# Start of a four-layer sequence kernel: the first batch's order, halved stack loads, and the second batch's transform ahead of the score units

## The reference, cut to what matters

```python
# layer 1 (stage A), per batch
q, k, v = u @ Wq.T + bq, u @ Wk.T + bk, u @ Wv.T + bv     # transposed to channel x time
q, k = dwconv(q), dwconv(k)                               # 3 taps
kv = k * v
y = irfft(rfft(kv) * rfft(ssm_kernel))[..., :L]
y = (y + kv * D_skip) * q
x = layernorm(u + y.T @ Wo.T + bo)
# layer 2 (stages C and B), per batch
attn = causal_softmax_attention(rmsnorm(x, ln1), Wq, Wk, Wv, Wo)    # 16 heads of 16
mod = 0.1 * tanh(attn @ A)
h = rmsnorm(x, ln2)
gate = silu(h @ W_in.T + mod * (h @ A) @ B)
x = layernorm(x + x + (gate * (h @ W_up.T)) @ W_down.T)
# layer 3 (stage D): cumulative sum of k*v, times q, projected; layernorm; layer 4: top 6 of 64 experts
```

## Time and profile before

| | us |
|---|---|
| median of three runs | 1110.93 |
| lowest, highest | 1100.03, 1113.92 |
| the profiled execution | 1113.63 |
| its span, first to last instruction | 1110.3 |
| TensorE busy in it | 1015.0 (91%) |
| mean granted TensorE clock | 0.964 |

### The profile page before, as it was taken

One profiled execution on the slowest core, in us unless ns is written; L12 is line 12 of the kernel. 1 busy time (PEld: TensorE's weight loads), 2 busy tenths in 40 slices (PEclk: granted clock), 3 DMA queues, 4 the chain that ended last, 5 costly groups with the idle time before them and its releaser, 6 DMA issues. The chain is left out here.

```text
span 1110.3 us, 20976 instructions
## 1 busy us (share of the span) xinstructions
PE 1015.0 (91%) x6531; PEld 826.7 (74%) x6531; DVE 618.6 (56%) x2071; ACT 338.1 (30%) x1035; POOL 458.9 (41%) x516
## 2 busy tenths in 40 slices
PE   8888999999999999999998998788998989898986
PEld 6665877877878878878776776576786868686874
DVE  4535466676776766667665563544344444444356
ACT  1235254263353453452542620011011101010333
POOL 2123142282291471551642814414455445455612
PEclk9899999999999999999999999898899989898999
DMA  9497590511412214004004101497496776768286
GB/s 364 137 253 146 150 282 11 129 40 52 94 47 79 58 44 115 32 34 119 30 26 119 50 10 49 172 347 266 140 296 210 226 229 201 232 201 272 81 317 222
DMA packets 102919, 163.28 MB, mean 147 GB/s; under 512 B 26865, under 2 KB 77010, under 8 KB 100434
## 3 DMA queue, kind: packets, MB, share of 16 engines
q1 hardware_dynamic: 85394, 113.31, 35.9%
q0 software_dynamic: 12288, 33.96, 8.2%
q10 hardware_dynamic: 5184, 15.36, 3.8%
HBM read 139.32 MB, written 61.87 MB: 181 GB/s over the span
## 5 line engine op out<-in xcount | busy, mean ns | idle before, releaser
L1154 ACT ACTIVATE prob<-bank,nmx 128x128 f32<-128x128 f32 (+1 forms) x256 | 104.9, 431 | 67.5 <-DVE nmx L1423 64.8
L612 POOL TENSOR_TENSOR prob<-prob,rec 128x512 f32<-128x512 f32 x96 | 99.6, 1045 | 54.5 <-DVE rec L1429 53.8
L1423 DVE TENSOR_REDUCE nmx<-bank 128x2 f32<-128x512 f32 (+1 forms) x96 | 65.3, 686 | 53.0 <-PE bank L843 43.1
L637 POOL DMA_INDIRECT x_rows<-x_copy,desti x84 | 85.2, 1015 | 18.3 <-issue 18.2
L1147 ACT ACTIVATE probT<-bank 128x512 f32<-128x512 f32 x96 | 58.0, 604 | 60.3 <-PE bank L707 58.0
L903 PE MATMUL bank<-h2T,w_up 128*128 128x256 f32 x256 | 66.4, 382 | 0.0
L905 PE MATMUL bank<-h2T,w_in 128*128 128x256 f32 x256 | 65.7, 379 | 0.0
L304 POOL TENSOR_TENSOR spare<-ones_row 128x1 f32<-128x1 f32 x49 | 9.4, 191 | 136.2 <-DVE d_cs L1654 75.0
L707 PE MATMUL bank<-cst,prob 128*128 128x128 f32 x384 | 60.2, 280 | 6.0 <-ACT probT L1147 4.5
L627 POOL TENSOR_TENSOR products<-z,products 128x512 bf16<-128x512 f32 x8 | 9.3, 1157 | 133.8 <-ACT products L1135 133.8
L971 PE MATMUL bank<-x3T,sh_gu 128*128 128x256 f32 (+1 forms) x192 | 49.3, 401 | 10.7 <-DVE sact L1540 6.6
(11 more groups left out here) (387 smaller groups left out, 2515.7 us busy)
## 6 DMA issues: line engine op xcount, KB each, us to landing
w_in<-in_e_w SPq DMA_DIRECT2D x20, 448.0 KB
w_up<-in_e_w SPq DMA_DIRECT2D x20, 448.0 KB
w_down<-in_e_w SPq DMA_DIRECT2D x20, 448.0 KB
products<-in_e_w SPq DMA_DIRECT2D x20, 448.0 KB
prob<-in_e_w SPq DMA_DIRECT2D x20, 448.0 KB
probT<-in_e_w SPq DMA_DIRECT2D x20, 448.0 KB
actT<-in_e_w SPq DMA_DIRECT2D x20, 448.0 KB
x_rows<-sgt SPq DMA_DIRECT2D x1, 8320.0 KB, 28.5
```

The source lines that it names most:

```text
L612: pool.tensor_tensor(p, p, r, ALU.mult).then_inc(S["b_scaled"], 1)
L637: pool.indirect_dma_start(x_rows, bass.IndirectOffsetOnAxis(ap=desti[:, n:n + 1].bitcast(U32), axis=0), rows[:, n // TOPK, :], None).then_ ...
L1154: i = act.activation(prob[:, u % PROBS, h * w:(h + 1) * w], psum(u % 2, h * w, (h + 1) * w), ACT.Exp, bias=nmx[:, u, h:h + 1], accum_out=s ...
L1423: dve.tensor_reduce(nmx[:, u, 0:512 // w], bank[:, u % 2, :].rearrange("p (h k) -> p h k", k=w), AX, ALU.max, negate=True).then_inc(S["b_m ...
```

## The change

Four things, all in the turns.

1. In the first batch VectorE combines the products into `Yre` and `Yim` right after making them, and GpSimd adds `bo` as soon as the forward transform is done. The first two operations on the matrix B (A3s) move behind the gating, the other two (A3t) behind C1. The idle matmuls become 2 before A5, 11 before C1, 2 before C2 and 8 before u0.
2. In the first batch `stack_up` loads each stack in halves of the heads: the first halves of q and of k (semaphore `st_half`), then the second halves. u0 waits for the first halves, u2 for the second.
3. In the second turn A2, A3a and A3b stand ahead of u0 on TensorE, with ScalarE's A2, VectorE's A3p and GpSimd's A3p moved likewise; A5 stands ahead of u7 instead of behind it.
4. In the six turns 2 to 7 VectorE's D5p stands ahead of its C2.

```diff
@@ ORDER, of some lists only
             "first": {
-                "dve": """A3p Aq A3s A4y A4z A5n A5o A6n A6o C1 C1s C2 Zk Zq""",
+                "dve": """A3p Aq A4y A4z A3s A5n A5o A6n A6o C1 A3t C1s C2 Zk Zq""",
...
             "second": {
-                "act": """u0 A2 u1 u2 u3 u4 u5 u6 u7 u8 u9 u10 u11 u12 u13 u14 B6a B6b C1 f0 f1 C2 f2 f3 C2v f4 f5 f6 Z1k f7 Z1v Z1q Z2""",
+                "act": """A2 u0 u1 u2 u3 u4 u5 u6 u7 u8 u9 u10 u11 u12 u13 u14 B6a B6b C1 f0 f1 C2 f2 f3 C2v f4 f5 f6 Z1k f7 Z1v Z1q Z2""",
@@ stack_up, SyncE
+            def half_of(t, half):
+                n = HEADS // KT * KT * L // 2
+                return t[:, half * n:(half + 1) * n]
...
                     for j, a in enumerate(first_parts):
                         parts = 3 if j < 2 else 2
-                        sp.dma_start(stack[n][j * 3 * HD:(j * 3 + parts) * HD].rearrange("p h k l -> p (h k l)"),
-                                     rows(t, a, a + parts)).then_inc(S[f"st_{n}"], 16)
+                        if first(b):
+                            sp.dma_start(half_of(stack[n][j * 3 * HD:(j * 3 + parts) * HD].rearrange("p h k l -> p (h k l)"), 0),
+                                         half_of(rows(t, a, a + parts), 0)).then_inc(S["st_half"], 16)
+                        else:
+                            sp.dma_start(stack[n][j * 3 * HD:(j * 3 + parts) * HD].rearrange("p h k l -> p (h k l)"),
+                                         rows(t, a, a + parts)).then_inc(S[f"st_{n}"], 16)
+                if first(b):
+                    for n, t, first_parts in (("q", q_parts, (0, 0, 0)), ("k", k_parts, (1, 2, 0))):
+                        for j, a in enumerate(first_parts):
+                            parts = 3 if j < 2 else 2
+                            sp.dma_start(half_of(stack[n][j * 3 * HD:(j * 3 + parts) * HD].rearrange("p h k l -> p (h k l)"), 1),
+                                         half_of(rows(t, a, a + parts), 1)).then_inc(S[f"st_{n}"], 16)
@@ A3, GpSimd
-                pool.wait_ge(S["a_pr"], b + 1)
-                pool.tensor_tensor(Yre, pr[0], pr[1], ALU.subtract).then_inc(S["a_Y"], 1)
-                pool.tensor_tensor(Yim, pr[2], pr[3], ALU.add).then_inc(S["a_Y"], 1)
-                if first(b):
+                if first(b):
+                    pool.wait_ge(S["a_X"], 2)
                     pool.wait_ge(S["ld_u"], 32)
+                else:
+                    pool.wait_ge(S["a_pr"], b + 1)
+                    pool.tensor_tensor(Yre, pr[0], pr[1], ALU.subtract).then_inc(S["a_Y"], 1)
+                    pool.tensor_tensor(Yim, pr[2], pr[3], ALU.add).then_inc(S["a_Y"], 1)
@@ scores, TensorE
                 if u == 0:
+                    need(pe, "b_act", b * FT)
                     if first(b):
-                        idle(22, 7)
-                    need(pe, "b_act", b * FT)
+                        idle(8, 7)
+                        pe.wait_ge(S["st_half"], 96)
+                if u == (2 if first(b) else 0):
                     pe.wait_ge(S["st_q"], (b + 1) * 48)
                     pe.wait_ge(S["st_k"], (b + 1) * 48)
@@ A3, VectorE
                 i.then_inc(S["a_pr"], 1)
+                if first(b):
+                    dve.wait_ge(S["a_pr"], 1)
+                    dve.tensor_tensor(Yre, pr[0], pr[1], ALU.subtract).then_inc(S["a_Y"], 1)
+                    dve.tensor_tensor(Yim, pr[2], pr[3], ALU.add).then_inc(S["a_Y"], 1)
```

More of the change, by code:

```diff
@@ L281, in build @@
             "a_q a_k a_v a_q_out a_k_out a_v_out a_qc a_kc a_kv a_kvT a_kvT_out a_X a_pr a_Y a_y a_z a_o a_r a_x1 "
[L282 removed]
+            "b_xn b_hT b_h1 b_h2 b_xT b_q b_k b_v b_first b_rest b_second b_third st_qw st_kw st_half st_q st_k b_v_out b_s b_max b_exp b_rec b_scaled b_pT b_pT_out b_pv b_mixed "
             "b_mod b_tanh b_mh b_gu b_gt b_act b_dn b_r b_x2 "
@@ L349, in build @@
                 "act": """u0 D1 u1 u2 D2k u3 u4 u5 u6 u7 u8 u9 D4 u10 S0 u11 S1 D4m u12 S2 u13 u14 B6a B6b C1 f0 f1 f2 C2 C2v f3 f4 f5 f6 Z1k f7 Z1v Z1q Z2""",
-                "dve": """u0 u1 u2 A3p u3 u4 D2v D2w u5 u6 D3n A4y u7 A4z D3o u8 u9 A5n u10 S0 A5o u11 A6n S1 D4m u12 A6o S2 B6b D4t SD C1 f0 D4k f1 f2 C2 f3 f4 D5p D4w D5h f5
+                "dve": """u0 u1 u2 A3p u3 u4 D2v D2w u5 u6 D3n A4y u7 A4z D3o u8 u9 A5n u10 S0 A5o u11 A6n S1 D4m u12 A6o S2 B6b D4t SD C1 f0 D4k f1 f2 D5p C2 f3 f4 D4w D5h f5
                         f6 Zk f7 Zq B8""",
@@ L794, in A5 @@
                 if first(b):
-                    idle(4, 7)
+                    idle(2, 7)
                 pe.wait_ge(S["a_z"], b * 2 + 2)
@@ L807, in C1 @@
                 if first(b):
-                    idle(8, 7)
+                    idle(11, 7)
                 pe.wait_ge(S["b_xn"], b + 1)
@@ L1347, in split_b, with split_rest @@
                     cs.link(dve.tensor_tensor(b_rest, b_b, b_part[0], ALU.subtract))
+            def split_rest(b):
+                if first(b):
                     cs.link(dve.tensor_copy(b_part[1], b_rest))
@@ L1613, in DTb @@
                 cr.link(dve.tensor_copy(expert_of.rearrange("p (c k) -> p k c", k=2), psum3(6)[:, :, 0:P]))
-            turns(dve, "dve", {"DTa": DTa, "DTb": DTb, "Zq": conv("q", q_sb, qc), "Aq": conv("q", q_sb, qc), "Zk": conv("k", k_sb, kc), "A3p": A3, "A3s": split_b, "C1s": stack_b, "A4y": gated(0), "A4z": gated(1), "A5n": A5, "A5o": A5o,
+            turns(dve, "dve", {"DTa": DTa, "DTb": DTb, "Zq": conv("q", q_sb, qc), "Aq": conv("q", q_sb, qc), "Zk": conv("k", k_sb, kc), "A3p": A3, "A3s": split_b, "A3t": split_rest, "C1s": stack_b, "A4y": gated(0), "A4z": gated(1), "A5n": A5, "A5o": A5o,
                         "A6n": A6, "A6o": A6o, "C1": C1, "C2": C2, **{f"u{u}": unit(u) for u in range(UNITS + 1)},
```

1 line of the change is left out of this document (removed), and 6 rows, old and new, of the table ORDER.

## The result

The changed kernel takes 1100.0 us, the median of 20 runs (1085.67 to 1108.58), against 1106.32 us of 20 runs of the kernel before. The ratio is 0.991, with a 95% interval of 0.988 to 0.994, or 10 us (6.9 to 13.3) of the kernel before's time; it leaves out executions more than 1.5% above the fastest of their kernel, 8 of the changed kernel's 20, and over all 20 of each the medians lie 6.3 us apart, a ratio of 0.994. So the gain is some 6 to 10 us. The forecast was 1099, 12 us less and no change beyond 2%. The profiled execution took 1098.68 us, with a span of 1096.8 us against 1110.3.

The account below looks back on a forecast made before the run. TensorE bounds steady turns; the first 68 us are a chain of dependent steps. Gains of 4.9 us at C1, 7.5 at u0, 11.8 at the inverse transform and 12.0 at f0 are cumulative: 1110.9 - 12 = 1099 us, range 1088 to 1109.

Parts of the forecast that it names:

- Convolution and combination: First batch up to the gating: combination until 24.2, convolution until 26.8, projection at about 29.1; its end 4.9 us earlier.
- From C1 to the stores: First batch: q's rest at 43.1 to 43.8, k's rest 6.2 us earlier, stores at about 45.5 instead of 51.72.
- The stacks: Loads ahead of u0: u0 at 60.5 instead of 67.95, 7.5 us earlier; halves worth only 1.2 us; u2 at 63.4.
- halves cost as much as wholes: Rival: second halves land at 75.5 and u2 waits for them, so nothing is gained, 1111 us; chance 0.06.
- The units: Second turn: ScalarE alone paces u0 to u4; inverse transform at 67.6, 11.8 us earlier; f0 at 93.0, 12.0 us earlier.
- Only the start counts: Rival: the units lose the transform as filler and wait; 7.5 us stay, 4.3 do not come, 1103.5 us; chance 0.15.
- 4.3 of them from this part: Second turn's units: of 11.8 us gained at the inverse transform, 4.3 come from moving the transform ahead of u0.
- A low clock around the transform: Rival: waits ahead of A3 lower TensorE's clock; transform 3.7 us longer, u0 at 64.2, 1102.8 us; chance 0.08.
- D5p: Turns 2 to 7: D5p ahead of C2 delays stores about 1.2 us, hidden by 4.5 us before unit 0; 0 taken.
- Slower than before: Rival: D5p delays TensorE in each of six turns; at 3 us each, 1117 us; chance 0.03.
- given back at the second fill: Rival: third turn's S0 waits for a fill whose landing did not move; all 12 us lost, 1111 us; chance 0.04.
- The sum: Whole kernel: -12 us, from 1113.6 to 1101.6 profiled, and from the three-run median 1110.9 to 1099 us.

Follow-up runs that it names:

- Run 2: The changed kernel with the first batch's combinations and the addition of bo back on GpSimd; the projection came 2.53 us later.
- run 1: The changed kernel with the first batch's order and idle matmuls as before; u0 5.89 us and the third turn 5.09 us later; one execution took 1092.66 us.
- run 7: The changed kernel with VectorE's C1s behind C2 (q's and k's rests) in the first turn; store 0.7 us earlier, third turn 2.1 us later.
- run 3: The changed kernel with stacks loaded whole and the transform left ahead of u0; u0 2.56 us later, third turn 0.93 us later.
- run 6: The changed kernel with D5p back behind f4 in turns 2 to 7; three turns took 78.37, 78.57 and 78.52 us.
- Run 8: The changed kernel with four idle matmuls in the two waits of the second turn's tail; third turn at 124.66, 2.44 us earlier.
- run 4: The changed kernel with the transform back behind u2, loads in halves; u0 at 56.21, inverse transform 1.65 us and third turn 0.18 us later.

## Why the prediction was right, step by step

- **Convolution and combination.** Right to 0.1 us: combination until 24.27, convolution until 26.76, gating at 26.79, projection at 29.10 and 1.89 us long. Run 2 shows the combination as the cause of the slow convolution, and that 2.53 of the 4.36 us that run 1 loses at the projection hang on it, though by the transform and its clock and not by the convolution. Run 1 shows the whole part at 5.1 to 5.9 us. That GpSimd's addition of bo costs nothing in its new place was an assumption. It started at 20.44, beside the products, and they took 0.69, 1.28 for two and 0.68, what they took before. By the Trainium skill (SBUF — State Buffer, "Who interferes with whom"), which leaves a VectorE instruction with at most one SBUF input, outside the two-port modes, out of the contention, it was to be so; this trace agrees.
- **From C1 to the stores.** C1 at 37.40, q's rest at 43.01 directly behind C1s, store at 45.63: each within 0.1 us. The 1.6 us that I called a cost of the move are real at q's rest, but run 7 avoided them and lost more than it gained.
- **The stacks.** u0 at 60.30 for 60.5, u2 at 63.32 for 63.4. Twelve loads landed 15.0 us after q's store, six whole ones 16.2 before, so the six more cost nothing and gave 1 us. The halves are worth more than the 1.2 us of the forecast: 2.6 us at u0 (run 3), and more in the old order. The figure of about 2 us for each DMA (the Trainium skill, DMA: Bandwidth & Descriptors, "Anatomy of one DMA"), which is given there for DMAs issued by GpSimd while these are issued by SyncE, would have put the landing 12 us later if such costs came one after the other; this trace shows that they do not add up. The rival *halves cost as much as wholes* fell with it.
- **The units.** The inverse transform started at 68.53, 0.9 us later than forecast. From u4 it took 2.28 us, where I had 1.5. In runs 1 and 6 the same steps, u4's scores and transposition and u3's values, took 1.49, so the pace was right, and the 0.8 us are the clock: these steps ran at half clock here (the row of 1.09 at 66.95). From the inverse transform to h2T,b_a another 1.4 us were gained, where I had 0.2; before, TensorE's clock was down in part of this stretch (0.82 from 96 to 100 us). So h2T,b_a is 12.27 us earlier.
- **The step that was mis-sized: f0 at 93.0 instead of 105.03, 12.0 us.** It took the steps between the units and f0 at their length of before. They ran at 1.2 GHz: 3.58 us for 1.83, and f0 gained 10.52 us. Run 8 had them back with four idle matmuls in the waits. Before, the clock had fallen behind the same wait, at 98.79 (1.09 us for four matmuls that take 0.63), and was back by 102.62; why it fell and came back later here isn't settled.
- ***Only the start counts.*** I gave it 0.15, and it is half true. Beside whole loads the move of the transform is worth 1.63 us at the inverse transform and 2.14 at h2T,b_a (2.8 by the estimate at full clock), so it does something. Beside halves it is 1.65 as measured, all of it accounted for by the slow transform of run 4, and 0.9 by the estimate. The step that failed is "4.3 of them from this part": it compared with a u0 that waits for whole loads. With u0 at 56.2 the time behind u0 in which TensorE now idles held the old order's work nearly as well. *A low clock around the transform* came true in 3 of the 11 executions that have it there (3 of the 9 with empty waits), though not in the changed kernel's, at 1.4 to 1.7 us and not 3.7; I had let every matmul of it run at half clock.
- **D5p.** The rest of q was ready at 183.2 and the value projection started at 183.5 without a wait: neutral in the steady turns, as forecast. The forecast missed the last turn but one, where the 4.5 us of cover that it counted on are not there and TensorE waits 1.06 us; run 6 shows that the next wait swallows this. *Slower than before* and *given back at the second fill* fell: the turns keep their 78.5 us and the lead stays between 10.9 and 11.0 us through them.
- **The sum.** -10.55 at the third turn, -11.4 behind u0 of the last turn but one, and in the medians -6.3, with a ratio that says -10. The profiled spans differ by 13.5 us; the last 2 us arise in the last turns and the experts, where the change does nothing and the clock varies between executions. What of them is chance wasn't tried. That 1099 met 1100.0 so closely is partly luck: the sum started from 1110.93, the median of three runs, and 20 runs of the same kernel gave 1106.32. The base was 4.6 us too high and the gain of 12 us too large by 2 to 6, and the two nearly cancel.

## What to carry to other kernels

In a chain of dependent steps with short waits, count every wait of TensorE as itself and, with a chance that a few executions show, as the matmuls behind it at half clock; filling such waits with one to three idle matmuls cost nothing here, and the run with them was 2.4 us ahead at the third turn. Before moving work out of an engine's way, look at what it will then run beside: VectorE's operations that read SBUF alone took half as long again and more beside GpSimd (1.28 to 1.94 and 2.06 us, and 0.73 to 2.72). Check a change of a loop's order in the first and the last pass too, where the work that hides it is missing. But a new wait in a trace is not yet a loss: look whether the next step would have waited anyway. And before two edits are priced one by one, ask whether each of them alone already removes the same wait.

## What the hardware showed that I had not expected

- TensorE's granted clock is not a function of the program. The transform behind waits of 1.02 and 0.69 us took 3.72 us in one execution and 5.41 in another whose instructions up to there were the same. The inverse transform of the first batch behind 2.36 us of idle time took 4.04, 5.37 and 5.72 in three executions, and behind 1.74 us 3.69 in all of eleven.
- Contention goes both ways and hits a bf16 operation with one SBUF input as well: TENSOR_SCALAR at 128x1024 took 0.49 us alone and 1.39 beside GpSimd, while GpSimd's 128x512 f32 product h2T went from 1.04 to 2.02. VectorE's product with one operand in PSUM beside GpSimd's addition kept its 0.69.
- 2 MB in twelve loads landed 14.4 to 15.4 us after the store that they wait for (eleven executions), in six loads after 16.1 to 16.9 (three). In the second batch six loads took 14.9 to 16.1 us, so more than the number of loads bears on it.
